# Two blocks of gated cross-attention and feed-forward: weights of the autocorrelation summed with their masking, and a new order of work around them

## The reference, cut to what matters

```python
# layer 0, cross-attention: autocorrelation, per head column
qf = jnp.fft.fft(q, axis=2); kf = jnp.fft.fft(k, axis=2)
corr = jnp.fft.ifft(qf * jnp.conj(kf), axis=2).real
topk = int(C * np.log(L))                       # 11
w, idx = jax.lax.top_k(corr.transpose(0, 1, 3, 2), topk)
w = jax.nn.softmax(w, axis=-1)
for i in range(topk):
    g = jnp.minimum(idx[:, :, None, :, i] + pos, L - 1)
    out = out + w[:, :, None, :, i] * jnp.take_along_axis(v, g, axis=2)
# layer 0, feed-forward: x @ W.T + b, and one of four low ranks (LoRA), chosen by a gate
scores = x @ gate_w.T + gate_b
out = jnp.einsum('bsd,od->bso', hidden_states, W) + b
final = jnp.sum(sel * routing_weights[:, :, None], axis=1)
# layer 1, cross-attention: 32 query heads, 8 key heads, rotary, mask, softmax
scores = jnp.einsum('bhgqd,bhkd->bhgqk', qg, k) / scale
w = jax.nn.softmax(masked, axis=-1)
out = jnp.einsum('bhgqk,bhkd->bhgqd', w, v)
# layer 1, feed-forward: a dense layer and an adapter made of a Fourier series
base = jnp.einsum('bsd,od->bso', x, W_base) + b_base
update = real_fourier_orthogonal_multiply(decoded).sum(axis=0)
```

## Time and profile before

| | us |
|---|---|
| median of 3 runs | 3265.72 |
| lowest and highest of them | 3260.21, 3273.69 |
| the profiled execution | 3258.55 |
| its span | 3256.7 |
| PE busy in it | 3118.1 (96%) |
| VectorE busy | 1991.4 (61%) |
| ScalarE busy | 1138.2 (35%) |
| GpSimd busy | 719.8 (22%) |
| granted TensorE clock, mean | 0.984 |

### The profile page before, as it was taken

The page is one execution under the profiler, slowest core; times in us unless marked ns, Lnnn a source line. Parts: engine busy times, 40 slices in busy tenths (PEclk is TensorE's granted clock), DMA queues, the critical chain, the costliest instruction groups (busy, mean ns, idle before and its releaser), DMA issues.

```text
span 3256.7 us, 42387 instructions
## 1 busy us (share of the span) xinstructions
PE 3118.1 (96%) x15200; PEld 2600.3 (80%) x15200; DVE 1991.4 (61%) x4623; ACT 1138.2 (35%) x2378; POOL 719.8 (22%) x585
## 2 busy tenths in 40 slices
PE   8999899998898979999999999999999999999899
PEld 7888677776676868888788888788888788888787
DVE  4333488888444467777766667666667666666432
ACT  4111356565212144444433333333333333333220
POOL 2422378786312122323100000000000000000221
PEclk9999999999999989999999999999999999999999
DMA  6332312112343456676674454454545455443621
GB/s 233 130 123 99 131 54 75 49 53 81 132 165 132 136 191 241 231 254 224 211 255 151 168 175 175 147 210 168 168 162 174 155 201 168 169 159 114 245 91 58
DMA packets 232827, 509.50 MB, mean 156 GB/s; under 512 B 23171, under 2 KB 58115, under 8 KB 232619
## 3 DMA queue, kind: packets, MB, share of 16 engines
q1 hardware_dynamic: 231466, 503.98, 44.4%
q10 hardware_dynamic: 1152, 2.82, 0.2%
HBM read 364.13 MB, written 142.61 MB: 156 GB/s over the span
## 4 chain that ended last, share of the span: by engine, by line
PE 62%; DVE 3%; DMA 1%; ACT 1%; issue 0%; POOL 0%; SPq 0%; DVEq 0%; ACTq 0%; POOLq 0%
PE PB L209 51%; PE PB L766 7%; PE PB L1271 3%; ACT at_ss L1252 1%; PE PB L737 1%; DMA xd<-at_xt 0%; DMA at_rawq<-in_wq 0%; PE PB L1185 0%; DVE at_ss L1263 0%; DVE at_xt L1307 0%; DVE at_ptl L197 0%; DVE at_st L214 0%; DMA at_wql<-wqd 0%; DVE at_ss L1246 0%; SPq L119 0%
## 5 line engine op out<-in xcount | busy, mean ns | idle before, releaser
L209 PE MATMUL PB<-at_woh,at_ah 128*128 128x512 f32 x1024 | 410.7, 401 | 6.3 <-POOL at_wol L197 3.2
L209 PE MATMUL PB<-at_hh,at_wqh 128*128 128x512 f32 x1024 | 401.7, 392 | 5.3 <-DMA at_wql<-wqd 3.4
L209 PE MATMUL PB<-at_hl,at_wqh 128*128 128x512 f32 x1024 | 401.1, 392 | 0.0
L209 PE MATMUL PB<-at_hh,at_wql 128*128 128x512 f32 x1024 | 399.9, 391 | 0.0
L209 PE MATMUL PB<-at_wol,at_ah 128*128 128x512 f32 x1024 | 399.8, 390 | 0.0
L209 PE MATMUL PB<-at_woh,at_al 128*128 128x512 f32 x1024 | 399.5, 390 | 0.0
L1252 ACT ACTIVATE at_ss<-at_ss,at_sm,at_bs 128x256 f32<-128x256 f32 x512 | 301.5, 590 | 274.2 <-DVE at_sm L1250 274.2
L1219 DVE TENSOR_TENSOR at_t<-PB,at_rt 128x512 f32<-128x512 f32 x128 | 88.5, 691 | 447.7 <-PE PB L209 447.7
L1307 DVE SCALAR_TENSOR_TENSOR at_xt<-PB,gt,at_xt 128x512 f32<-128x512 f32 x256 | 190.6, 746 | 114.5 <-PE PB L209 114.5
L194 ACT ACTIVATE at_ah<-PB 128x512 fp32r<-128x512 f32 x128 | 76.5, 598 | 480.7 <-PE PB L209 480.7
L209 PEld LDWEIGHTS PB<-at_hh,at_wqh 128*128 128x128 f32 x1024 | 193.7, 189 | 43.0 <-issue 5.7
(11 more groups left out here) (269 smaller groups left out, 7301.0 us busy)
## 6 DMA issues: line engine op xcount, KB each, us to landing
at_wqh<-wqd SPq DMA_DIRECT2D x96, 512.0 KB, 3.6
at_wql<-wqd SPq DMA_DIRECT2D x96, 512.0 KB, 4.5
at_woh<-wod SPq DMA_DIRECT2D x48, 1024.0 KB, 5.1
at_wol<-wod SPq DMA_DIRECT2D x48, 1024.0 KB, 7.6
at_rawq<-in_wq SPq DMA_DIRECT2D x32, 512.0 KB, 6.4
wqd<-at_wqh SPq DMA_DIRECT2D x32, 512.0 KB, 8.4
wqd<-at_wql SPq DMA_DIRECT2D x32, 512.0 KB, 8.4
at_rawo<-in_wo SPq DMA_DIRECT2D x32, 512.0 KB, 6.4
```

What stands on the lines that cost most here:

```text
L209: e.matmul(o, a, b, start=i == 0, stop=last), *(waits if i == 0 else ()), *w, mark=last)
```

## The change

Two parts are made together.

In the autocorrelation `topk` and `weights` lose te, its exponential and its sum: the four STTs give the sums of what they write through an accumulator, into tz, and the reciprocal follows them. The negation of the largest goes from VectorE to ScalarE. The low part of the queries (ql) is made by VectorE for unit 0, and from unit 2 on waits for the four STTs of the unit before its own. The low part of the last unit's weights is made by VectorE.

```diff
             def split_q(u):
                 pf = (S[u - 1]["P1"],) if u else ()
-                S[u]["q"] = split(qh[:, :, :], ql[:, :, :], xn[:, :, :], S[u]["xn"] + pf, l_on="gpsimd")
+                weighed = S[u - 2]["s"][0] if u > 1 else []
+                eh = op("scalar", lambda e: e.activation(qh[:, :, :], xn[:, :, :], ACT.Copy), *S[u]["xn"], *pf)
+                el = op("gpsimd" if u else "vector", lambda e: e.tensor_tensor(ql[:, :, :], xn[:, :, :], asf(qh[:, :, :]), ALU.subtract),
+                        eh, *S[u]["xn"], *pf, *weighed)
...
-                n = op("vector", lambda e: e.tensor_scalar(tz[:, 0, :], t16[:, :, 0], -1.0, None, ALU.mult), a[3])
+                n = op("scalar", lambda e: e.activation(tz[:, 0, :], t16[:, :, 0], ACT.Copy, scale=-1.0), a[3])
...
-                f = op("vector", lambda e: e.tensor_tensor(te[:, :, 0:TOPK], t16[:, :, 0:TOPK], t16[:, :, 0:1].to_broadcast([P, 4, TOPK]), ALU.subtract), c[3])
-                m = op("vector", lambda e: e.memset(t16[:, :, TOPK:16], NEG), f)
+                m = op("vector", lambda e: e.memset(t16[:, :, TOPK:16], NEG), c[3])
...
             def weights(u):
-                g = op("scalar", lambda e: e.activation(te[:, :, 0:TOPK], te[:, :, 0:TOPK], ACT.Exp), f)
-                h = op("vector", lambda e: e.tensor_reduce(tz[:, 1, :], te[:, :, 0:TOPK], AX, ALU.add), g)
-                h = op("vector", lambda e: e.reciprocal(tz[:, 2, :], tz[:, 1, :]), h)
                 s_ = [op("vector", lambda e, k=k: e.scalar_tensor_tensor(
-                    out=w0[:, k, :], in0=w2[:, k, :], scalar=NEG, in1=w1[:, k, :], op0=ALU.is_equal, op1=ALU.mult), r[k], x_[k]) for k in V4]
+                    out=w0[:, k, :], in0=w2[:, k, :], scalar=NEG, in1=w1[:, k, :], op0=ALU.is_equal, op1=ALU.mult,
+                    accum_out=tz[:, 1, k:k + 1]), r[k], x_[k]) for k in range(4)]
+                h = op("vector", lambda e: e.reciprocal(tz[:, 2, :], tz[:, 1, :]), s_[3])
...
-                    d["spW"] += split(sh[j], sl[j], pa[j], (d["sumW"][j],) + pf, l_on="gpsimd")
+                    d["spW"] += split(sh[j], sl[j], pa[j], (d["sumW"][j],) + pf, l_on="gpsimd" if u < NU - 1 else "vector")
```

The other part moves work without changing what it computes. In the first periods the split of unit 0's products is recorded ahead of kv's tail, and unit 2's context ahead of the norm of batch 1. In f0 `lora_in`, the gates, the bias and the norms of tiles 2 and 3 move into the loop over c, and the pieces of the adapter come one step earlier:

```diff
                 if a == 0:
+                    split_products(a)
                     yield
...
                 if a == 1:
+                    prepare_c(2)
                     stats(1)
                     prepare_q(2)
                     split_q(2)
...
-                if a + 1 < NU:
+                if a + 1 < NU and a != 1:
                     prepare_c(a + 1)
...
-            lora_in(0)
...
-                if c == 1:
+                if c == 0:
+                    lora_in(0)
+                if c == 2:
                     gates_of(0)
-                if c == 4:
+                if c == 5:
                     lora_flip(0)
-            scale_bias()
+                    scale_bias()
+                    add_bias(0)
+                    add_bias(1)
+                if c == 6:
+                    norm(2)
+                    norm(3)
...
             piece(-1)
-            norm(2)
-            norm(3)
-            add_bias(0)
-            add_bias(1)
...
-                elif 4 <= i < 4 + C:
-                    c = i - 4
+                elif 3 <= i < 3 + C:
+                    c = i - 3
```

```diff
-                        take(qn + 1, t)
+                        takes.append((4 * n + 4 + p // 2, qn + 1, t))
...
+                if u + 4 < H:
+                    fetch_wq(u + 4)
                 if u + 2 < H:
                     keep_wq(u + 2)
-                if u + 4 < H:
-                    fetch_wq(u + 4)
-                if u % 4 == 1 and u > 4 and u // 4 + 1 < NG:
+                if u % 4 == 1 and u // 4 + 1 < NG:
                     load_kv(u // 4 + 1)
+                if u == 2:
+                    for t in range(4):
+                        take(0, t)
...
+                while takes and takes[0][0] < u:
+                    take(*takes.pop(0)[1:])
...
+                if w == 31 and more:
+                    project(u + 1)()
+                    load_wq(u + 3)
                 rest = project(u + 2) if u + 2 < NU and not late else None
+                if u < 4:
+                    weigh(u)
...
-                if u < NU:
+                if 4 <= u < NU:
                     weigh(u)
...
                 if late:
-                    project(u + 2)()
+                    flip(qn + 1, 3, 0, nq[3])
+                    flip(qn + 1, 3, 1, nq[3])
...
                 room["x"] = yield
-                for t in range(4):
-                    load(t, *room["x"])
+                load(2, *room["x"])
+                load(3, *room["x"])
+                room["w47"] = yield
                 norm(0, *room["x"])
                 norm(1, *room["x"])
-                room["w47"] = yield
```

42 lines of the change are left out of this document (21 added, 21 removed).

## The result

The changed kernel takes 3210.03 us (median of 4 runs, 3208.48 to 3212.80) against 3262.97 before (4 runs, 3259.47 to 3273.69): ratio 0.9828, interval 0.9809 to 0.9846. I had predicted 3201, range 3176 to 3236. The profiled execution takes 3212.8 with a span of 3211.0, so between the two profiles 45.75 us went, where my sum had 64.3; between the medians 53. Both kernels make 15,200 matmuls in nearly the same order, so a stretch of PE's work can be compared by the start of its nth matmul, as in the table further down.

A forecast was written before the change was run, and what follows sets the result against it. PE, busy 96% of the span, was taken as the bound, so only its idle time and lower-clock stretches could be won. Terms summed to -64.3 us, giving 3201 us from the median of 3265.72; range 3176 to 3236.

The forecast's parts named there:

- First periods: Autocorrelation's first periods: unit 0's ql on VectorE and earlier products and preparation remove PE waits; -12.5 us (-5 to -15).
- Steady periods: Autocorrelation, 427 to 768 us: a shorter path to the weights brings long periods to 24.3; -27 us (-15 to -33).
- the wait for the STTs: Autocorrelation's long periods: STTs fall from 3.57 to four times 0.417 because ql waits for them; 1.9 us each.
- even and odd within 0.5 us: Sign expected in the profile after: the autocorrelation's even and odd periods within 0.5 us of each other, near 24.3.
- The accumulating STT: Autocorrelation's weights: each STT keeps 0.417 us and adds a 0.083 accumulator read, 0.3 for four.
- Rival B: Autocorrelation: the accumulating STT is slower, up to twice 0.417 us; 12 us less gain, total 3213; chance 0.15.
- rival A: Autocorrelation: GpSimd becomes the bound, periods fall only to about 26; -3 to -15 us, total 3220; chance 0.22.
- 768 to 852: F0's start, in us of the profile: the low-rank product's wait of 8.65 only moves; 0 (-4 to +4).
- First flips: 1013 to 1030 us: PE's wait of 5.12 and 1.4 of lower clock go, pieces one tile earlier; -6.5 (-2 to -8).
- Start of the cross-attention: 1085 to 1200 us: project(0) moved, -2 (-3 to 0); rawq loaded earlier for the 12.63 wait, -6 (-12 to 0).
- Block ends: Cross-attention's block ends: deferred loads remove the wait for wql, -5.3 us (-6 to 0); other changes there, -1.
- End: Kernel's end: wait of 3.71 goes, two x tiles ahead of wo cost +2.4; -4 us (-8 to +3).

The follow-up runs named there:

- The parts alone: Two kernels: the one before with only the autocorrelation's edits, 3227.12 us; the changed kernel with those edits taken back, only the order of work new, 3251.13 us.
- gate_undone: The changed kernel without the wait of ql for the four STTs of the unit before; 3207.98 us.
- weights_alone: The kernel before with only the autocorrelation's edits (te gone, accumulating STTs, negation on ScalarE, ql behind the STTs); 3227.12 us, ratio 0.987.
- f0_as_before: The changed kernel with the order of work at f0's start as before, the adapter's pieces still one step earlier; 3205.95 us.
- pieces_as_before: The changed kernel with the adapter's pieces one step later, as in the kernel before; 3218.03 us.
- gate_alone: The kernel before with one edit: ql on GpSimd waits for the four STTs of the unit before; 3252.49 us.
- Mended: The changed kernel with f0's start reordered, wq fetched ahead of stores only for u < 8, f1's tiles 2 and 3 loaded behind wo's last slice; 3202.14 us.
- f1_loads_late: The changed kernel with loads of f1's first two tiles back behind those of the first weights and wo's last slice; 3212.07 us.
- f0_new_order: The changed kernel with another order at f0's start: bias scaled and added first, then low-rank weight split, then flip; 3209.65 us.

## Why the prediction was right, step by step, and where it was off

- **First periods.** -12.5 predicted, -13.6 measured (P4 of unit 1 starts at 413.37 instead of 426.99). Right in size, partly by luck. The parts alone give -6.3 for the weights and -7.9 for the order (420.73 and 419.05), where my terms gave the weights 1.2 (unit 0's ql) and the order 11.3. The weights alone already bring the wait of 4.26 down to 1.50.
- **Steady periods.** -27 predicted, -26.6 measured (314.8 for 341.5). The size was right and one term's reason was not, so the close agreement is partly luck. I gave the wait for the STTs 1.9 of 4.1 us a long period; gate_undone gives it 0. The STTs are out of ql's way because the chain ahead of them got shorter. tz, which I took by its median of 1.15, has waits of 4.9 too, and they made odd periods long; I had the maximum in the earlier trace rows and didn't ask how often it comes. Of my seven long periods six were even and gained 3.2 each, where I had 3.5, and the seventh was an odd one with the long tz and gained 4.2. Nor do all meet PE's own work at 24.3: that is 23.8, and the even ones stop at 24.7, where L538 still paces the transposes. So the sign "even and odd within 0.5 us" did not come.
- **The accumulating STT.** I took 0.417 and 0.083; it is 0.417 and 0.078, and four take 1.6 us together where they took 1.4 alone without it, 0.2 more for my 0.3. Rival B is out. The rule that I cited from the Trainium skill's "Vector Engine (DVE) Microarchitecture Reference" (section 7, half throughput with two sources in SBUF that aren't bf16, since no read port is left for the accumulator) does not show here: the median is the same 0.417 as without an accumulator. The slowest of 64 takes 0.594: the first of each four takes 0.55 to 0.59 in units 1 to 14, for a reason that no run shows. The measurement decides.
- **GpSimd takes over (rival A).** It is busy 264 of 315 us and PE has no wait for it: it does not.
- **768 to 852.** 0 predicted, -4 to +4. Up to PE's 3600th matmul -2.6, then +5.8 to the 4200th, +3.2 in all. The first comes with the weights (-3.4 in weights_alone), and against that kernel the order costs 6.7 here. In the 5.8 the order of f0's start has 3.3 (f0_as_before) and the pieces 3.0 (pieces_as_before), each within 2 us of noise. I had priced the moved wait and the earlier pieces at nothing; the wait of 8.65 came back as three with 14.1 us and a clock of 0.87 for 0.93. The number is within its bounds, the step failed.
- **First flips.** -6.5 predicted, -5.5 measured in its stretch against the profile of before (-7.4 by pieces_as_before), and 4.4 net, since a piece one tile earlier costs 3.0 where it lands.
- **Start of the cross-attention.** -8 predicted (-2 and -6), -5.8 measured. at_rawq comes earlier (ScalarE waits 6.40 for 11.52), and PE's waits of 12.63 and 7.82 become 6.04 and 6.13, both for at_ql. VectorE is what holds it now. Ahead of the first stands an addition of two SBUF tiles that takes 2.12 for 0.69 beside GpSimd's split (1098.41), ahead of the second at_ql itself takes 2.20 for 0.68 (1132.72); in both, the multiplications of the softmax and the split of at_pth stand ahead of at_ql too.
- **Block ends.** -5.3 and -1 predicted. The wait for wql did go, and the list of takes did it (+2.8 without). But at the first end a wait of 0.99 became 3.08. The two profiles have 188.6 and 187.5 there, while weights_alone and gate_alone, with the old order, take 186.3 and 186.4: no gain is shown. The other two ends are 2.5 slower in the profile (125.7 and 125.2 for 123.7 and 124.7), where kernels with the same code differ by up to 3.3 and 2.0. This step failed: the wait that I priced went, and its gain was given back at the first end. Mended, which fetches behind the stores from unit 8 on, still waits 2.71, so the stores are not the whole of it; the rest stays open.
- **End.** -4 predicted, -0.1 measured between the two profiles. The three kernels with the old end take 198.0 to 200.9 (mean 199.5) and the nine with the new one 195.0 to 198.1 (mean 196.8), so -2.6 is the better figure. The 3.71 went, since the norms no longer hold up at_pth. The two tiles ahead of wo's slice, priced at +2.4, cost 3.0 (3.30 here, 0.26 in f1_loads_late). A wait of 1.6 stands where it was 1.5, so that estimate of mine did not come.

Together: the autocorrelation gave what was forecast, 40.2 for 39.5, and everything behind it 5.6 for 24.8 in the profiles. The forecast failed in size in the re-ordered stretches. In f0's start, in the first units, at the first block's end and at the end, the wait that I had priced shrank or went, and another instruction of the same queue, or a transfer, was next.

## What to carry to other kernels

A tiny instruction can be the gate: look at the maximum and at the count of a line's durations, not at the median alone, and move one that another engine's long instructions block to a free engine. A wait that is moved is not gone: list what stands in each queue between the new place and the instruction that the critical engine wants, all of it, before you price the move at nothing. Comparing kernels by the start of their nth matmul turns one profile each into a ledger by stage. It tells edits of a few us apart, once kernels with the same code in a stretch have shown how far they differ there. When a load is late, find the issue whose landing ends the wait before you name what stands ahead of it: two loads of the same name stand close together at the end here. And compare a period with one of its own kind; a wait in slices too short for a bracket shows only in the group's length.

## What the runs showed of the hardware that I had not expected

- A VectorE TENSOR_SCALAR with one input of 128x4 takes 0.17 us alone. Beside a run of GpSimd's 128x512 subtractions it ended, in all 60 cases, 0.02 to 0.03 after one of them: mostly the first it met (1.16 in the median), in 11 cases the last of the run (4.4 to 4.9). VectorE's instructions with PSUM as an input (0.68 each) and its MAX8 (0.41) beside the same run are not longer.
- An accumulating SCALAR_TENSOR_TENSOR costs its 0.417 and a read of 0.078 that lies nearly beside the next: the later ones of four start 0.345 apart.
- GpSimd is held up as well: two of its additions, 4.73 us in the changed kernel, took 6.58 in f0_new_order, where VectorE's subtraction (2.32) and clearing (2.77) of SBUF tiles ran beside them.
